# Attention scores with two of three partial products on TensorE and the third by a block transpose on VectorE

## The reference, cut to what matters

```python
kx = modulated_linear(x, s, k_aff_w, k_aff_b, k_w, k_b)
kx = kx.reshape(B, N, H, D)                 # H = 16 heads, D = 32
q = k = v = kx
scores = jnp.einsum('bnhd,bnjd->bnhj', q, k) / math.sqrt(D)
A = jax.nn.softmax(scores, axis=-1)
out = jnp.einsum('bnhj,bnjd->bnhd', A, v).reshape(B, N, F)
out = modulated_linear(out, s, o_aff_w, o_aff_b, o_w, o_b)
```

## Time and profile before the change

| | |
|---|---|
| median of 3 runs | 870.54 us |
| the profiled execution | 869.47 us, its span 867.6 us |
| TensorE matmul (PE) | 836.8 us, 96% |
| TensorE weight load (PEld, overlaps PE) | 731.9 us, 84% |
| VectorE (DVE) | 646.7 us, 75%, 1067 instructions |
| ScalarE (ACT) | 487.6 us, 56% |
| GpSimd (POOL) | 605.7 us, 70% |
| mean DMA rate | 110 GB/s |

### The profile page before, as it was taken

How to read it: one execution, slowest core, us unless ns; L and a number is a source line. 1 busy time by engine, 2 the same in 40 slices (tenths; PEclk the granted TensorE clock), 3 DMA queues, 4 the chain that set the end, 5 groups by cost and what they waited for, 6 DMA issues and landing times.

```text
span 867.6 us, 19685 instructions
## 1 busy us (share of the span) xinstructions
PE 836.8 (96%) x7456; PEld 731.9 (84%) x7474; DVE 646.7 (75%) x1067; ACT 487.6 (56%) x851; POOL 605.7 (70%) x766
## 2 busy tenths in 40 slices
PE   5996999999999999999999999999999999999997
PEld 5853888988889898888989898888988898898986
DVE  3589778778786867678797877679797767677652
ACT  3567555565656465465656556465647546464531
POOL 2367998778786767768776866668787775756472
PEclk9998999999999999999999999999999999999999
DMA  8972233424343333525243332424343342323110
GB/s 277 419 268 62 71 91 105 126 63 150 83 151 81 98 93 86 128 51 158 71 149 89 107 93 69 127 68 145 83 123 91 87 117 49 104 68 83 47 50 25
DMA packets 104365, 95.55 MB, mean 110 GB/s; under 512 B 72880, under 2 KB 78160, under 8 KB 102608
## 3 DMA queue, kind: packets, MB, share of 16 engines
q1 hardware_dynamic: 95056, 69.26, 27.7%
q0 software_dynamic: 4608, 16.78, 7.1%
q10 hardware_dynamic: 4608, 8.25, 2.8%
HBM read 69.60 MB, written 8.40 MB: 90 GB/s over the span
## 4 chain that ended last, share of the span: by engine, by line
PE 88%; DVE 5%; DMA 2%; POOL 2%; issue 1%; ACT 1%; ACTq 0%; another core or an unknown queue 0%; DVEq 0%; POOLq 0%
PE acc L405 43%; PE tok L405 28%; PE att L405 8%; PE xp L558 6%; PE xp L405 3%; DMA kb<-in_kb 1%; DVE stg_e L1284 1%; DMA pgb<-in_pw,pidx 1%; DVE raw_k L1170 0%; DVE W1xl L1274 0%; POOL op0l L1706 0%; DVE qt L1290 0%; POOL W2l L1710 0%; DVE q L1297 0%; DVE BD L1185 0%
## 5 line engine op out<-in xcount | busy, mean ns | idle before, releaser
L1706 POOL TENSOR_TENSOR op1l<-ytmp,op1h 128x512 fp32r<-128x512 f32 x64 | 89.8, 1403 | 20.1 <-ACT op1h L912 19.6
L1652 POOL TENSOR_TENSOR xlo<-xraw,xhi 128x512 fp32r<-128x512 f32 x31 | 40.5, 1306 | 68.0 <-ACT xhi L804 68.0
L405 PE MATMUL acc<-op0h,W1xh 128*128 128x256 f32 x256 | 75.8, 296 | 1.4 <-DVE op0l L1376 1.1
L405 PE MATMUL acc<-op1h,W1th 128*128 128x256 f32 x256 | 75.0, 293 | 0.0
L405 PE MATMUL acc<-op1h,W1hh 128*128 128x256 f32 x256 | 73.7, 288 | 0.0
L405 PE MATMUL acc<-op0h,W1sh 128*128 128x256 f32 x256 | 73.7, 288 | 0.0
L405 PE MATMUL acc<-op1h,W1tl 128*128 128x256 f32 x256 | 72.4, 283 | 0.0
L405 PE MATMUL acc<-op1l,W1hh 128*128 128x256 f32 x256 | 72.4, 283 | 0.0
L405 PE MATMUL acc<-op1l,W1th 128*128 128x256 f32 x256 | 72.4, 283 | 0.0
L405 PE MATMUL acc<-op0h,W1sl 128*128 128x256 f32 x256 | 72.4, 283 | 0.0
L405 PE MATMUL acc<-op1h,W1hl 128*128 128x256 f32 x256 | 72.4, 283 | 0.0
(11 more groups left out here) (269 smaller groups left out, 3005.2 us busy)
## 6 DMA issues: line engine op xcount, KB each, us to landing
xsq<-in_x SPq DMA_DIRECT2D x32, 256.0 KB, 3.1
xb<-in_x SPq DMA_DIRECT2D x32, 256.0 KB, 3.0
out<-xb SPq DMA_DIRECT2D x32, 256.0 KB, 2.4
BD<-q SPq DMA_DIRECT2D x124, 64.0 KB, 2.1
BD<-v SPq DMA_DIRECT2D x124, 64.0 KB
xraw<-in_xT SPq DMA_DIRECT2D x30, 256.0 KB, 3.0
ring<-in_k_wT ACTq DMA_DIRECT2D x6, 256.0 KB, 3.3
dmb<-dm_rows SPq DMA_DIRECT2D x6, 256.0 KB, 3.9
```

What stands on the lines that cost most here:

```text
L405: return e.matmul(o, a, b, start=start, stop=True, skip_group_check=True)
L1652: e.tensor_tensor(xlo[:, :, :], (xraw1 if g == 1 else xraw)[:, :, :], xhi[:, :, :].bitcast(F32), ALU.subtract).then_inc(s["xlo"], 1)
L1706: e.tensor_tensor(op[slot]["l"][:, :, half(g)], four(ytmp[YT[n, g][0]]), op[slot]["h"][:, :, half(g)].bitcast(F32), ALU.subtract).then_inc ...
```

## The change

TensorE no longer multiplies the lo weights with q hi. The product that is left out, lo.hi, is the transpose of hi.lo inside every 32x32 block, since a token's scores are symmetric; the mask in SE is symmetric too. VectorE transposes SE inside its 32x32 blocks into ET, adds SE onto the even columns of att as before, and then adds ET. ET is also what a_sum writes and a_T reads, so that from the second group on VectorE waits until a_T of the group before is done (aTr). The new semaphore lT orders the two additions and the transpose. Its place among the semaphores is taken from c_L, whose one wait now goes to c_bd.

```diff
             def scores(g):
@@ TensorE
                     q = q12[:, j // 2, :, j % 2, :]
-                    mm(both, diag(j, 0), q, start=(j % 8 == 0))
-                    i = mm(both[:, :, 0], diag(j, 1), q[:, :, 0])
+                    i = mm(both, diag(j, 0), q, start=(j % 8 == 0))
                     if j % 8 == 7:
                         i.then_inc(s["S"], 1)
@@ VectorE
                 if n == "t":
                     e.wait_ge(s["c_two"], 32)
-                    e.wait_ge(s["c_L"], 1)
+                    e.wait_ge(s["c_bd"], 2)
@@ VectorE
             def score_sum(g):
 
                 e.wait_ge(s["Sc"], 2 * g + 2)
-                e.tensor_tensor(high, high, SE[:, :], ALU.add).then_inc(s["Ss"], 1)
+                if g:
+                    e.wait_ge(s["aTr"], g)
+                e.transpose(ET[:, :], SE[:, :]).then_inc(s["lT"], 1)
+                e.tensor_tensor(high, high, SE[:, :], ALU.add).then_inc(s["lT"], 1)
+                e.wait_ge(s["lT"], 2 * g + 2)
+                e.tensor_tensor(high, high, ET[:, :], ALU.add).then_inc(s["Ss"], 1)
@@ GpSimd
             for n in "tshmnr":
                 i = e.memset(L[n][:, :, :], 0.0)
-            i.then_inc(s["c_L"], 1)
+            i.then_inc(s["c_bd"], 1)
```

## The result

The changed kernel takes 880.27 us (median of 4 runs, 879.47 to 882.90) beside 870.95 us for the kernel before (4 runs, 870.13 to 872.37): a ratio of 1.0113, with an interval from 1.0090 to 1.0135. The forecast was 883.6 us with a range of 873 to 892.5. The profiled execution of after took 882.90 us with a span of 881.1 us, that of before 869.47 and 867.6 us; the profiled one of after is the longest of its four, so differences between the two traces (+13.5 us) are larger than those between the medians (+9.3 us). I come back to that.

What follows compares the result with a forecast made beforehand. TensorE was taken to bound the kernel, with VectorE turning late in places. Profiled 869.5 + 13.6 (scores(a+2)) - 2.7 (scores(b)) + 2.2 (prologue) = 882.6, as a median 883.6 us; range 873 to 892.5.

Steps and rivals of the forecast that it cites:

- The removed work, 0.54 us a burst: TensorE's scores: 16 fewer matmuls a group at 33.6 ns save 0.54 us, 17.2 us in all if nothing is late.
- D: VectorE's score_sum: the new transpose and second addition make it 1.33 us longer a group, up to 1.7 with the slow transpose.
- Rival (c): VectorE's new transpose has the slow form, D = 1.68 us: 892.7 us, chance 0.12.
- x_one, +0.95 and +1.0: scores(a+2): x_one queues behind the additions and TensorE waits; eight iterations lose 0.95 us, six lose 1.0, sum +13.6 us.
- rival (a): TensorE stays the bound and VectorE's idle time takes the additions: 853.3 us, chance 0.08.
- k = 1: scores(b) there: TensorE already waits 1.3 us for u_make; half of D taken as loss, +0.7 us.
- scores(b): 15 iterations: u_make just covered in ten, -0.54 us each; with the five others the sum is -2.7 us.
- k = 3, 7 and 11: scores(b) there: u_make has only 0.28 us idle before it, so u_T comes 0.4 us later each time.
- k = 15: scores(b) there: u_make has 0.50 us idle before it, so u_T comes 0.8 us later.
- Prologue: Before the iterations: VectorE runs without a pause, so score_sum(1) and score_sum(2) come late, +2.2 us; group 0 costs nothing.
- rival (e): Stalls take TensorE's clock down: half speed for some 4 us after each of 14, 2 us each; 912 us, chance 0.02.

Runs made afterwards that it cites:

- mid_only: Kernel before with the change made for the odd groups from 3 on alone (scores(b)); 864.37 us, ratio 0.9919.
- pe_only: Changed kernel with VectorE's old single addition and no transpose, so lo.hi is left out altogether; 861.08 us, ratio 0.9877 against the kernel before.
- x_first: Changed kernel with x_one(b) put ahead of last_stats(pb) on VectorE; 885.08 us, ratio 1.0151 against the kernel before.
- dve_only: Changed kernel with TensorE still multiplying lo.hi, so that it counts twice; 886.97 us, ratio 1.0177 against the kernel before.
- mid_again: The same kernel as mid_only, run once more beside mid_13; 864.63 us, ratio 0.9928 against the kernel before.
- mid_13: Kernel before with the change made for the odd groups 5 to 29 alone; 864.68 us, ratio 0.9923.
- end_only: Kernel before with the change made for the even groups from 4 on alone (scores(a+2)); 883.25 us, ratio 1.0135.
- mid_double: mid_13 with the transpose done twice, the second waiting for the first; 873.02 us, ratio 1.0023 against the kernel before.
- no_add2: Changed kernel without the second addition, the transpose kept but unused; 867.28 us, ratio 0.9953 against the kernel before.

## Why the prediction was right, and where its numbers were off

The place, the size and the cause of the main loss were right: fourteen waits for x_one, for the reason given. Two smaller terms have the right number for a wrong reason, or can't be told from the spread of single executions. They follow in the order of the forecast.

**The removed work, 0.54 us a burst: right.** The burst takes 0.56 us in the chain, and a middle is shorter by 0.54. The removed matmuls had half the columns of those that stay and cost as much, so the columns don't set the pace (by columns the saving would have been 0.36 us). That the weight loads set it is likely and not shown by a run. The Trainium skill (TensorE: Matmul & The Clock Gate, "Wait — 56ns, not 53.3ns?") has about 25 ns between small matmuls as the least there can be, by which a burst would be worth an estimated 0.40 us; the runs stay above it with 0.54 / 16 = 33.8 ns.

**D, 1.33 us: right to within 0.1.** In a middle (mid_only's k = 9) the transpose starts at 508.99 and the second addition at 510.33, 1.34 us. At the end of the iteration the transpose starts at 540.16 and the maximum at 542.19, 2.03 us where it was 0.70, 1.33. Rival (c), the slow transpose, is out.

**x_one, +0.95 and +1.0: right in place and size, though the way there had an error.** The ends lose 0.92 and 0.98 us, 13.3 us in sum for the 13.6 of the forecast. I had 14 waits of 1.5 us; they are 1.0 us. The difference is that TensorE can't be 0.54 us early at x_T(a): a_lo holds the output projection, as in pe_only (540.12 to 540.27 in after). What TensorE does not win ahead of a later wait costs nothing, so the sum kept its value. It would have been wrong by 3.8 us for rival (a), whose 853.3 us, with both additions free, was out of reach: pe_only, which lacks the transpose and the second addition, has 861.1, and without the 4.1 us that its k = 1 falls short some 857.

**scores(b): right in nine of the ten plain iterations, wrong by a step in k = 3, 7 and 11.** In mid_only all middles from k = 2 to 14 are 0.54 us shorter up to values(b), in after all but k = 12. For k = 3, 7 and 11 I had +0.4 us each; mid_only shows -0.01 at u_T in k = 3 and 7 and +0.19 in k = 11, on top of the -0.54, and after -0.01, -0.01 and +0.22. The step that failed is that u_make would end 1.33 - 0.28 us later. In k = 7 the rows of VectorE and POOL in before are:

```profile
413.93 0.70 DVE L1318 TENSOR_TENSOR att<-att,SE 128x512 f32<-128x512 f32 x1 [0.93 <-ACT SE L841]
...
415.39 0.69 DVE L1324 TENSOR_TENSOR SE<-att,small 128x512 f32<-128x512 f32 x1
```

```profile
415.23 1.31 POOL L1706 TENSOR_TENSOR op1l<-ytmp,op1h 128x512 fp32r<-128x512 f32 x1
416.49 1.07 POOL L1670 TENSOR_TENSOR SE<-SE,wT 128x512 f32<-128x512 f32 x1
```

and in mid_only, which is 2.17 us earlier at scores(b) of that iteration:

```profile
411.13 0.71 DVE L1324 STREAM_TRANSPOSE ET<-SE 128x512 f32<-128x512 f32 x1 [0.68 <-ACT SE L842]
...
413.92 0.69 DVE L1333 TENSOR_TENSOR SE<-att,small 128x512 f32<-128x512 f32 x1
```

```profile
414.69 1.06 POOL L1679 TENSOR_TENSOR SE<-SE,wT 128x512 f32<-128x512 f32 x1 [0.69 <-DVE SE L1333]
```

Two things had been left out. ScalarE had SE ready 0.63 us earlier (411.13 + 2.17 = 413.30 against 413.93), as its copy follows the shorter burst here, not only by 0.15. And POOL had been busy until 416.49, while the subtraction was done at 416.08: 0.4 us of slack further down. So the scaling moved by 414.69 + 2.17 - 416.49 = +0.37 us instead of 1.33, and 0.28 us of that vanished before u_make. I had looked at the two ends of the chain and not at the engines between them. k = 15 is as forecast: +0.72 us net for +0.8.

**k = 12 in after** is 0.09 us longer up to values(b) and not 0.54 shorter. TensorE waits there for e_second, which stands on VectorE behind the statistics (L1372) of rows that POOL fetches with an indirect DMA. TensorE's row, POOL's first step on these rows in after, and the same step in mid_only:

```profile
682.63 1.22 PE L405 MATMUL att<-e,BD 128*128 128x64 f16 x32 [0.48 <-DVE e L1343]
...
678.26 1.30 POOL L1695 TENSOR_TENSOR pgb<-z,pgb 128x512 f32<-128x512 f32 x1 [2.58 <-DMA pgb<-in_pw,pidx]
...
661.49 1.29 POOL L1700 TENSOR_TENSOR pgb<-z,pgb 128x512 f32<-128x512 f32 x1 [1.01 <-DMA pgb<-in_pw,pidx]
```

The DMA is issued 1.95 us after the start of scores(b) in both. x_first has the late landing too (a wait of 2.60 us), dve_only with all of D has not (k = 12 up to values(b) as before). Why it came late is not shown.

**k = 1: the number was right and the reason wrong.** Values(3) came 0.74 and u_T 0.08 us later, +0.82 for the +0.7 that I had taken as half of D. But D is not felt there: POOL's scaling starts 7.43 to 7.49 us after the start of scores(3) in all thirteen traces, with D and without. pe_only, which has no D, loses 0.74 us, and mid_again, which has it, wins 0.4. What moves is again the landing of the indirect DMA. POOL's first step on its rows in before, after, pe_only and mid_again:

```profile
121.73 1.29 POOL L1691 TENSOR_TENSOR pgb<-z,pgb 128x512 f32<-128x512 f32 x1 [0.57 <-DMA pgb<-in_pw,pidx]
...
124.22 1.29 POOL L1695 TENSOR_TENSOR pgb<-z,pgb 128x512 f32<-128x512 f32 x1 [1.43 <-DMA pgb<-in_pw,pidx]
...
121.26 1.29 POOL L1690 TENSOR_TENSOR pgb<-z,pgb 128x512 f32<-128x512 f32 x1 [1.34 <-DMA pgb<-in_pw,pidx]
...
122.77 1.29 POOL L1700 TENSOR_TENSOR pgb<-z,pgb 128x512 f32<-128x512 f32 x1 [0.21 <-DMA pgb<-in_pw,pidx]
```

The wait is 0.86 us longer in after than in before, and u_T is 0.82 later. Six of the seven traces with a short burst in k = 1 have the late landing and none of those with the old burst, so the burst may have a part in it; that is open.

In after's trace scores(4) then came another 1.44 us later, behind a stretch in which TensorE's clock stood at half, 1.2 GHz (two stretches: us, busy times, granted clock, share of DMA, GB/s):

```profile
130.00:132.00 2.00, 0.55 (x4) 0.51 (x4) 0.28 (x1) 1.38 (x4) 1.92 (x5) 0.78 0.25 53
132.00:134.00 2.00, 2.00 (x7) 1.71 (x6) 1.97 (x4) 1.63 (x4) 2.00 (x2) 0.50 0.56 137
```

This is rival (e) once instead of fourteen times, with some 3.4 us at half speed (from the shares of these stretches and 0.87 in the next) and 1.4 us of cost, where (e) had supposed 4 and 2. Whether the three executions without a trace had it too is not known.

**Prologue: +2.2 us forecast, not to be told from the spread.** The first matmul of the first W1 comes 1.6 us later in after, but 1.2 of them are there at the start of scores(0), ahead of anything that changed. In mid_only, mid_again, mid_13, end_only and mid_double, whose prologues are that of before, the same place lies at -0.3, +1.4, +2.2, +0.3 and -1.1 us.

Adding up the steps of the two traces, forecast in brackets: the fourteen ends +13.3 us (+13.6), the fifteen middles with what lies between them and the ends -2.8 (-2.7), the prologue +1.6 (+2.2), the slow clock +1.4 (0): 13.5 for the 13.56 between the last landmarks. The middles agree only in sum. k = 3, 7 and 11 were 2.8 us too dear in the forecast (+1.2 for three times -0.54). Against that stand 0.6 us of k = 12 and, in this trace, small shifts at u_T(a) and scores(a+2), mostly 0.04 to 0.10 us each, the largest 0.34, which give back 1.8 us that I had not counted; mid_only had nearly none of them, mid_again 0.1 to 0.2 us in each plain iteration. I take them for the edge that mid_double found, with D now on one side of TensorE's arrival and now on the other; no wait in the profiles shows it.

The medians are 9.3 us apart, where the forecast had 13.1, and 4.2 less than the traces: after's profiled execution lies 2.6 us above its own median (882.90 to 880.27), and before's 1.5 us below its own (869.47 to 870.95). I had corrected for the latter with 1.07 us on top of the trace, which kept the size of the change as it was in one execution. Against the medians the forecast of 883.6 is 3.3 us too high, and the clock, k = 1, k = 12 and the prologue show that a single execution varies by that much; which term the other executions have less of, no trace here shows.

## What to carry to other kernels

An addition on an engine that has a quarter of its time free is priced by its place in that engine's queue: the same 1.33 us cost 0.9 us net where the next result stood directly behind it, and nothing in twelve of fifteen places where other engines' work lay between. Make such a change only where it is covered; mid_only, the odd groups alone, keeps the whole product and is 0.8 and 0.7% faster than the kernel before in two batches, and faster than the changed one. Price a term by an execution only as far as executions agree: two profiles of the same kernel differed by 1.1 us in one iteration and by 1.7 us in the prologue. And when a piece is moved ahead in a queue, price every result that it is moved past, down to those that other engines make from it: x_first traded fourteen waits for others worth more.

## What the runs showed of the hardware that was not expected

- **The slow and the fast transpose differ by how the input lies, not by the buffers.** ET<-SE takes 691 ns at L1319 and 1081 ns at L1351, both 128x512 f32. The second reads with a stride, and nothing else in their operands differs.
- **An addition behind a transpose that it doesn't wait for starts 0.59 us after it** (540.16 to 540.75 in after; 0.64 in mid_only's k = 9). An instruction of this size that waits for the one before it starts 0.70 to 0.73 us after it (510.33 to 511.06 there): about a tenth of a microsecond for each such dependence.
- **An indirect DMA landed up to 2 us apart in the same place.** Behind the start of scores(25) in k = 12, POOL's first step on its rows starts at 6.76 us in before, 7.27 in mid_only and 8.84 in after, with the DMA issued at 1.91 to 1.95 in all three.
- **The clock fell after short waits, but not always.** At u_T of k = 1 TensorE had waited 1.12 us for e_second and, 2.9 us later, 1.46 us for u_make in after, and the clock was at half (1.2 GHz) from within the second wait, about 131.1 by the share of its stretch, until about 134.5: matmuls of W2 came every 0.43 us instead of every 0.23. pe_only (1.05 and 1.45 us of waits, clock 0.50 from 128 to 134) and x_first had it too. But mid_only, with 0.98 and 1.45 us, and no_add2, with 1.18 and 1.45 us, kept the full clock there, and none of the fourteen waits of 1.0 us at x_T took it down. Why the one pair fell and the other did not stays open; before, with one wait of 1.35 us, did not fall.
